# Layer 1 attention of a four-part transformer kernel: where VectorE's remainder of the turned probabilities stands in its queue, in the last step of a light head

## The chip, the cores and the metric

The kernel runs on one core of a Trainium2 chip. The core has TensorE (PE in the profile) for matrix products, VectorE (DVE), ScalarE (ACT), GpSimd (POOL) and SyncE (SP), which issues DMAs here. Each engine works through a queue of its own in the order in which the program put the instructions there, and engines wait for each other with semaphores. The metric is the device time of one execution in microseconds (us); lower is better. The time of the kernel before is 1416.83 us, the median of three runs (1416.50 to 1417.45).

## What is computed

Two transformer layers on 4 sequences of 256 tokens with 512 features, in float32. Only the attention of layer 1 is touched:

```
q = einsum('bsd,de->bse', x, wq).reshape(B, S, 32, 192)
k, v = 32 heads of 128 each out of x @ wkv
scores = einsum('bqhd,bkhd->bhqk', q[..., :128], k) * scale
scores = where(causal, scores, -1e30)
probs = softmax(scores, axis=-1)
attn = einsum('bhqk,bkhd->bqhd', probs, v)
out = einsum('bse,ed->bsd', attn, wo)
x = layernorm(x + out)
```

Before it stand layer 0 (attention, a gated feed-forward network) and behind it the last feed-forward part with its eight small experts.

## The kernel before

**Layout.** Tokens lie in 128-row tiles, two tiles to a sequence. A float32 operand of a product is held as two parts, a rounded one (`hi`) and the remainder (`lo`), and a product is three matmuls, hi x hi, hi x lo and lo x hi (`matmul3`, lines 106 to 108).

**Steps.** `programs` writes the attention of layer 1 as five functions, one for each engine. Each runs over 16 groups (`gr`), with two heads in each (`hd` 0 and 1, so head `h = 2 * gr + hd`) and four steps in each head (`t`, one for each sequence; the step number is `s = 4 * h + t`). Groups 1 to 14 are a loop, `Fori(1, NG - 1)`; group 0 and group 15 are written out apart. `light(gr, hd)` is true for the even head of the two groups that are written out, so for heads 0 and 30. In these, TensorE has less to do in a step than in the loop.

**What a step does.** The softmax of step `s + 1` is made while step `s` is at its products:

- TensorE: `scores(s + 1)` (lines 2240, 2241, 106 to 108 into `c_bs`), `turn(s)`, three transposes of the probabilities into `c_bt` (line 75), then products of the next head's queries and keys (`c_bx`, `c_by`), or of values or outputs (`c_bv`), and at the end `values(s)` (into `c_bo`). `turn(s)` waits for `s_norm`, which ScalarE raises when it has normalised the probabilities. `values(s)` waits for `s_tlo`, which VectorE raises when it has made the remainder of the turned probabilities.
- VectorE: `out_sum(s - 1)` (line 1999), `maxes(s + 1)`: the mask and the negated row maxima (lines 1977, 1978, 1981, 1983, 1985), `outs(s - 1)` (line 2006), `probs(s)`: the remainder `pt[1] = bt - pt[0]` (line 1993), `inverse(s + 1)` (line 1989), then parts of the next head.
- ScalarE: `out_rest(s - 1)` (line 1865), `probs(s)`: the rounded part `pt[0]` out of `bt` (line 1860), `outs(s - 1)` (line 1871), `exps(s + 1)` (line 1847), which waits for the maxima, `normalise(s + 1)` (line 1855), which waits for the reciprocals of `inverse`. In head 31 it also splits the weights of the last part there (line 2389).
- GpSimd splits the weights of the next heads.

Each function's text is the order of its engine's queue; no scheduler moves anything. In the last step (`t == 3`) of a light head VectorE's `probs(s)` already stands ahead of `outs(s - 1)`, behind `maxes(s + 1)`. These steps are `s = 3` (head 0) and `s = 123` (head 30).

The two places where such a step runs lie at 528 to 533 us and 1317 to 1322 us of the span.

Of the kernel before, what the change touches and what calls it, by code (L numbers as in the profile page):

```python
# [67 lines left out]
def f32(ap):  # L68

    return ap.bitcast(F32)  # L70
# [28 lines left out]
def has(x, n):  # L99

    return not isinstance(x, int) or 0 <= x < n
# [1443 lines left out]
class Attention1:  # L1545
# [128 lines left out]
    def programs(self, k, before, after, ffn0, end):  # L1674
# [8 lines left out]
        NSTEP = NB * NH  # L1683
# [41 lines left out]
        def in_last(gr):  # L1725
            return isinstance(gr, int) and gr == NG - 1

        def light(gr, hd):
            return isinstance(gr, int) and gr in (0, NG - 1) and hd == 0
# [241 lines left out]
        def vector(dve):  # L1971
            def maxes(s, t):


                dve.wait_ge(s_smm, s + 1)
                bank = bs[t % 2]
                dve.tensor_tensor(s0, bank[:, 3 * P:4 * P], mask, ALU.add).then_inc(s_mk, 1)
                dve.tensor_tensor(bank[:, 2 * P:3 * P], bank[:, 2 * P:3 * P], mask, ALU.add)\
                   .then_inc(s_mk, 1)
                dve.wait_ge(s_mk, 3 * s + 1)  # L1980
                dve.tensor_tensor(s0, bank[:, 0:P], s0, ALU.add).then_inc(s_mk, 1)
                dve.wait_ge(s_mk, 3 * s + 2)
                dve.tensor_reduce(nmax[t % 2][:, 1:2], bank[:, P:3 * P], AX, ALU.max, negate=True)
                dve.wait_ge(s_mk, 3 * s + 3)
                dve.tensor_reduce(nmax[t % 2][:, 0:1], s0, AX, ALU.max, negate=True).then_inc(s_max, 1)  # L1985

            def inverse(s, t):
                dve.wait_ge(s_exp, s + 1)
                dve.reciprocal(rinv[t % 2][:, :], rsum[t % 2][:, :]).then_inc(s_inv, 1)  # L1989

            def probs(s):
                dve.wait_ge(s_thi, s + 1)
                dve.tensor_tensor(pt[1], bt[:, 0:3 * P], f32(pt[0]), ALU.subtract).then_inc(s_tlo, 1)

            def out_sum(s, t):

                dve.wait_ge(s_orest, s + 1)
                out = bo[t % 2][:, P:2 * P]
                dve.tensor_tensor(out, out, o1, ALU.add).then_inc(s_osum, 1)  # L1999

            def outs(s, hd, b):
                dve.wait_ge(s_ohi, s + 1)
                tok = slice(b * S, (b + 1) * S)
                if isinstance(s, int) and s == 4 * (NH - 1):
                    dve.wait_ge(s_sumlo, 3 * NH)
                dve.tensor_tensor(out_home(s, 1, hd, tok), bo[b % 2][:, 0:S], f32(out_home(s, 0, hd, tok)),
                                  ALU.subtract).then_inc(s_olo, 1)

            def value_lo(n, b, bank):
                dve.wait_ge(s_vhi, n + 1)  # L2010
                dve.tensor_tensor(v[1][:, 2 * b:2 * b + 2, :], bank[:, :].rearrange("p (a n) -> p a n", a=2),
                                  f32(v[0][:, 2 * b:2 * b + 2, :]), ALU.subtract).then_inc(s_vlo, 1)

            def add_out(n, j, bank):

                dve.wait_ge(s_omm, n + 1)
                dve.tensor_tensor(res[:, j, :], bank[:, :], res[:, j, :], ALU.add).then_inc(s_oadd, 1)  # L2017

            def add_last(i):
                if i >= 14:  # L2020
                    dve.wait_ge(s_oadd, before_last + i - 1)
                add_out(before_last + i, last_tiles[i][1], last_banks[i])

            def last_stats(j):

                after.stats(dve, j, (s_oadd, before_last + last_tiles.index((B, j)) + 1))

            def total(h, i):

                n = (0, 2, 1)[i]  # L2030
                dve.wait_ge(s_y, 3 * h + i + 1)
                dve.wait_ge(s_copy, 3 * h + n + 1)
                if i == 1:
                    m = dve.tensor_tensor(y[:, n, :], by[:, :], y[:, n, :], ALU.add)
                else:
                    m = dve.scalar_tensor_tensor(out=y[:, n, :], in0=by[:, :], scalar=SCALE1, in1=y[:, n, :],  # L2036
                                                 op0=ALU.mult, op1=ALU.add)
                m.then_inc(s_sum, 1)

            def key_lo(h, par):  # L2040
                dve.wait_ge(s_khi, h + 1)
                dve.tensor_tensor(qk[par][:, 1, 1, 0:HALF], bx[:, :], f32(qk[par][:, 0, 1, 0:HALF]),
                                  ALU.subtract).then_inc(s_klo, 1)
# [59 lines left out]
            def unit(gr, hd):  # L2103
                h = 2 * gr + hd
                for t in range(NB):
                    s = 4 * h + t
                    if has(s - 1, NSTEP):
                        out_sum(s - 1, (t - 1) % 4)
                    if hd == 1 and t and has(gr + 1, NG):
                        value_lo(4 * gr + 4 + t - 1, t - 1, bv)  # L2110
                    if hd == 0 and t == 0 and not (isinstance(gr, int) and gr == 0):
                        value_lo(4 * gr + 3, 3, bv)
                    if has(s + 1, NSTEP):
                        maxes(s + 1, (t + 1) % 4)
                    few = light(gr, hd)
                    if few and t == 3:
                        probs(s)
                    if has(s - 1, NSTEP):
                        outs(s - 1, hd if t else 1 - hd, (t - 1) % 4)
                    if has(s, NSTEP) and not (few and t == 3):  # L2120
                        probs(s)
                    if few and t == 2:
                        key_lo(h + 1, 1 - hd)
                    if has(s + 1, NSTEP):
                        inverse(s + 1, (t + 1) % 4)
                    if hd == 0 and not in_last(gr) and has(gr - 1, NG):
                        add_out(8 * (gr - 1) + 2 * t, 2 * t, bv)
                    if t == 2 and has(h + 1, NH) and not few:
                        key_lo(h + 1, 1 - hd)
                    if t < 3 and has(h + 1, NH):  # L2130
                        total(h + 1, t)
                    if hd == 0 and not in_last(gr) and has(gr - 1, NG):
                        add_out(8 * (gr - 1) + 2 * t + 1, 2 * t + 1, bv if t < 3 else by)
                    if in_last(gr):
                        steps = last_steps.get((hd, t), ())
                        if hd == 1 and t == 2:
                            add_last(steps[0])
                            steps = steps[1:]
                        if hd == 1 and t >= 2:
                            for j in (2 * t - 4, 2 * t - 3):  # L2140
                                last_stats(j)
                            if t == 3:
                                after.spread(dve, 0, 4)
                        for i in steps:
                            add_last(i)

            def epilogue():
# [8 lines left out]
                end.vector(dve, (s_oadd, NT * NG))  # L2156

            sweep(dve, prologue, unit, epilogue)

        def tensor(pe):  # L2160
# [675 lines left out]
```

## Time and profile before

| | |
|---|---|
| Median of three runs | 1416.83 us (1416.50 to 1417.45) |
| The profiled execution, its own time | 1415.87 us |
| Its span, first to last instruction | 1414.1 us |
| Attention of layer 1, group 0 / loop / group 15 | about 511 to 560 / 560 to 1304 / 1304 to 1345 us |
| Mean granted TensorE clock | 0.999 of full speed |

The page gives busy time of each engine, the chain of work that ended last, and groups of instructions with their mean duration and the idle time ahead of them. A timeline view lists instructions of an engine by their start. In square brackets it gives the idle time of the engine ahead of an instruction and whose end it waited for. Matmuls overlap: the distance from start to start, and not the duration, is what each costs. The same holds on VectorE, where the next instruction's start can lie up to a tenth of a microsecond ahead of the end of the one before.

### The profile page before, as it was taken

How to read it: one execution, taken by the hardware profiler on the slowest of the kernel's cores; microseconds unless marked ns; L12 is line 12 of the kernel's file. 1: busy time of each engine (PE TensorE's matmuls, PEld its weight loads, DVE VectorE, ACT ScalarE, POOL GpSimd, SP SyncE). 2: the span in 40 equal slices, each digit the busy share in tenths (PEclk: the TensorE clock that was granted, in tenths of full speed). 3: DMA queues.
4: the chain of work that ended last, by engine and by line, in shares of the span. 5: the costliest groups of instructions: out<-in, count | busy, mean ns of one | idle time of the engine just before them, and what ended most of it. 6: DMA issues, size and time to landing. Idle time of an engine off the chain costs nothing.

```text
span 1414.1 us, 30207 instructions
## 1 busy us (share of the span) xinstructions
PE 1400.2 (99%) x8769; PEld 1236.6 (87%) x8769; DVE 1017.3 (72%) x2528; ACT 891.2 (63%) x2445; POOL 774.0 (55%) x828
## 2 busy tenths in 40 slices
PE   9999999999999999999999999999999999999998
PEld 7898889888788878889889889889889889889887
DVE  5999999999968875665665665665665665665776
ACT  5888888888555576555556556556556556556711
POOL 3555555555040467765765765665665665665521
PEclk9999999999999999999999999999999999999999
DMA  5533333322445301111101011001002001000201
GB/s 197 169 95 95 95 95 95 94 66 51 134 135 164 97 31 61 31 31 59 30 30 59 30 30 59 30 30 59 30 30 59 30 30 59 30 30 30 83 16 46
DMA packets 56155, 92.60 MB, mean 65 GB/s; under 512 B 6064, under 2 KB 27312, under 8 KB 56112
## 3 DMA queue, kind: packets, MB, share of 16 engines
q1 hardware_dynamic: 55968, 91.93, 21.3%
q8 instruction: 23, 0.38, 0.1%
q14 instruction: 20, 0.16, 0.0%
q10 hardware_dynamic: 144, 0.13, 0.0%
HBM read 81.82 MB, written 2.10 MB: 59 GB/s over the span
## 4 chain that ended last, share of the span: by engine, by line
PE 94%; DVE 2%; ACT 1%; issue 1%; POOL 1%; DMA 1%; SPq 0%; POOLq 0%; DVEq 0%; ACTq 0%
PE c_bv L106 8%; PE c_bv L108 7%; PE c_bv L107 7%; PE c_bx L106 5%; PE h_bo L944 5%; PE c_bx L108 4%; PE c_bx L107 4%; PE c_by L106 4%; PE c_by L108 4%; PE c_by L107 4%; PE h_bo L1447 3%; PE a_acc L1447 3%; PE h_bt L75 3%; PE h_bs L106 2%; PE c_bt L75 2%; PE h_bs L108 2%
## 5 line engine op out<-in xcount | busy, mean ns | idle before, releaser
L618 POOL TENSOR_TENSOR h_pr<-h_pr,h_rinv 128x512 f32<-128x512 f32 x128 | 133.2, 1041 | 136.7 <-DVE h_rinv L769 134.3
L1778 POOL TENSOR_TENSOR c_qk<-g_y,c_qk 128x512 fp32r<-128x512 f32 x96 | 124.0, 1292 | 147.3 <-ACT c_qk L1890 140.6
L1629 POOL TENSOR_TENSOR b_sw_lo<-b_slots,b_sw_hi 128x512 fp32r<-128x512 f32 (+1 forms) x128 | 148.1, 1157 | 10.2
L1627 POOL CAST b_sw_hi<-b_slots 128x512 fp32r<-128x512 f32 (+1 forms) x128 | 72.6, 567 | 143.6 <-DMA b_slots<-in_w_qk 125.5
L106 PE MATMUL c_bv<-b_wv_hi,g_xT_hi 128*128 128x256 f32 x496 | 138.8, 280 | 0.2 <-DVE g_xT_lo L1183 0.2
L108 PE MATMUL c_bv<-b_wv_hi,g_xT_lo 128*128 128x256 f32 x496 | 138.8, 280 | 0.0
L107 PE MATMUL c_bv<-b_wv_lo,g_xT_hi 128*128 128x256 f32 x496 | 138.7, 280 | 0.0
L1999 DVE TENSOR_TENSOR c_bo<-c_bo,g_wo 128x128 f32<-128x128 f32 x128 | 38.3, 300 | 122.3 <-ACT g_wo L1865 117.6
L1890 ACT ACTIVATE c_qk<-g_y 128x512 fp32r<-128x512 f32 x96 | 60.7, 632 | 96.5 <-DVE g_y L2036 67.1
L671 ACT ACTIVATE h_pr<-h_bs,h_nmax 128x256 f32<-128x256 f32 x256 | 119.3, 480 | 2.5 <-DVE h_nmax L764 2.4
L1855 ACT ACTIVATE c_pr<-c_pr,c_rinv 128x128 f32<-128x128 f32 (+1 forms) x256 | 101.8, 448 | 9.1 <-DVE c_rinv L1989 9.1
L1847 ACT ACTIVATE c_pr<-g_wo,c_nmax 128x128 f32<-128x128 f32 x128 | 51.5, 403 | 84.3 <-DVE c_nmax L1985 84.3
L107 PEld LDWEIGHTS c_bv<-b_wv_lo,g_xT_hi 128*128 128x128 f32 x496 | 93.1, 188 | 4.7
L106 PEld LDWEIGHTS c_bv<-b_wv_hi,g_xT_hi 128*128 128x128 f32 x496 | 93.0, 187 | 4.7 <-DVE g_xT_lo L1183 0.3
L1609 POOL TENSOR_TENSOR b_slots<-b_slots 128x256 f32<-128x256 f32 x128 | 93.8, 755 | 2.5
L108 PEld LDWEIGHTS c_bv<-b_wv_hi,g_xT_lo 128*128 128x128 f32 x496 | 93.1, 188 | 0.0
L2017 DVE TENSOR_TENSOR g_res<-c_bv,g_res 128x512 f32<-128x512 f32 x103 | 71.2, 692 | 27.2 <-PE c_bv L108 27.2
L764 DVE TENSOR_REDUCE h_nmax<-h_bs 128x2 f32<-128x512 f32 x128 | 87.5, 684 | 0.0
L773 DVE TENSOR_TENSOR h_pt_lo<-h_bt,h_pt_hi 128x512 fp32r<-128x512 f32 x128 | 87.2, 681 | 0.2
L1860 ACT ACTIVATE c_pt<-c_bt 128x384 fp32r<-128x384 f32 x128 | 62.9, 491 | 35.3 <-PE c_bt L75 31.5
L1865 ACT ACTIVATE g_wo<-c_bo 128x128 f32<-128x128 f32 x128 | 35.3, 276 | 77.3 <-PE c_bo L2262 77.3
L106 PE MATMUL c_bv<-b_wo_hi,c_oT 128*128 128x512 f32 x200 | 81.4, 407 | 0.0
(480 smaller groups left out, 5140.2 us busy)
## 6 DMA issues: line engine op xcount, KB each, us to landing
f_wi<-in_w_ffn SPq DMA_DIRECT2D x66, 256.0 KB, 2.7
b_slots<-in_w_qk SPq DMA_DIRECT2D x64, 256.0 KB, 3.0
a_w<-in_w_head SPq DMA_DIRECT2D x28, 352.0 KB, 2.9
h_part<-in_w_ffn SPq DMA_DIRECT2D x32, 264.0 KB, 2.7
b_raw_v<-in_w_v SPq DMA_DIRECT2D x16, 512.0 KB, 4.5
b_raw_o<-in_w_o SPq DMA_DIRECT2D x16, 512.0 KB, 4.5
h_o_mix<-h_o_hi SPq DMA_DIRECT2D x62, 128.0 KB, 2.2
b_ffn_w<-in_w_ffn SPq DMA_DIRECT2D x4, 576.0 KB, 5.6
```

Of the source, the lines that this page charges most:

```text
L106: pe.matmul(out, w[0], x[0], start=start, stop=False, skip_group_check=True)
L107: pe.matmul(out, w[0], x[1], start=False, stop=False, skip_group_check=True)
L108: return pe.matmul(out, w[1], x[0], start=False, stop=stop, skip_group_check=True)
L618: pool.tensor_tensor(pr[b][:, :, :], pr[b][:, :, :], rinv[b][:, :][:, :, None].to_broadcast([P, 2, S]), ALU.mult)\
L671: m = act.activation(pr[b][:, i, :], bs[b % 2][:, i * S:(i + 1) * S], ACT.Exp, bias=nmax[b][:, i:i + 1], accum_out=rsum[b][:, i:i + 1])
L764: dve.tensor_reduce(nmax[b][:, :], bs[b % 2][:, :].rearrange("p (a n) -> p a n", a=2), AX, ALU.max, negate=True).then_inc(s_max, 1)
L773: dve.tensor_tensor(pt[b][1][:, :, :], bt[b % 2][:, :].rearrange("p (a n) -> p a n", a=2), f32(pt[b][0][:, :, :]), ALU.subtract).then_inc( ...
L1447: m = pe.matmul(out, a, b, start=start and i == 0, stop=stop and i == len(pairs) - 1, skip_group_check=True)
L1609: pool.tensor_tensor(slot(out), slot(a), slot(b), op).then_inc(self.s_comb, 1)
L1629: pool.tensor_tensor(self.sw[1][:, a:b], self.slots[:, a:b], f32(self.sw[0][:, a:b]), ALU.subtract)\
L1778: pool.tensor_tensor(lo, src, f32(hi), ALU.subtract).then_inc(s_sumlo, 1)
L1855: m = act.activation(x[:, cols], x[:, cols], ACT.Identity, scale=rinv[t % 2][:, i:i + 1])
```

## The change

In the last step of a light head, VectorE's `probs(s)` (one instruction, line 1993 in both kernels, with its wait for `s_thi`) is placed ahead of `maxes(s + 1)` (five instructions) instead of behind it. No instruction is added or removed, and no other engine's order changes.

```
                         value_lo(4 * gr + 3, 3, bv)
-                    if has(s + 1, NSTEP):
-                        maxes(s + 1, (t + 1) % 4)
                     few = light(gr, hd)
                     if few and t == 3:
                         probs(s)
+                    if has(s + 1, NSTEP):
+                        maxes(s + 1, (t + 1) % 4)
                     if has(s - 1, NSTEP):
                         outs(s - 1, hd if t else 1 - hd, (t - 1) % 4)
```

`few and t == 3` holds twice: in group 0, step 3, and in group 15, step 123. VectorE's queue at the first place, in the kernel before (`c_bs0` are the scores of step 4, `c_bt` the turned probabilities of step 3, `c_bo0` the attention output of step 2, `g_wo` holds scratch):

```order
399 L1999 TENSOR_TENSOR c_bo0<-c_bo0,g_wo 128x128
400 L1977 TENSOR_TENSOR g_wo<-c_bs0,g_wo 128x128
401 L1978 TENSOR_TENSOR c_bs0<-c_bs0,g_wo 128x128
402 L1981 TENSOR_TENSOR g_wo<-c_bs0,g_wo 128x128
403 L1983 TENSOR_REDUCE c_nmax0<-c_bs0 128x1
404 L1985 TENSOR_REDUCE c_nmax0<-g_wo 128x1
405 L1993 TENSOR_TENSOR c_pt<-c_bt,c_pt 128x384
406 L2006 TENSOR_TENSOR c_oT<-c_bo0,c_oT 128x256
407 L1989 RECIPROCAL c_rinv0<-c_rsum0 128x2
```

And in the changed one:

```order
399 L1999 TENSOR_TENSOR c_bo0<-c_bo0,g_wo 128x128
400 L1993 TENSOR_TENSOR c_pt<-c_bt,c_pt 128x384
401 L1977 TENSOR_TENSOR g_wo<-c_bs0,g_wo 128x128
402 L1978 TENSOR_TENSOR c_bs0<-c_bs0,g_wo 128x128
403 L1981 TENSOR_TENSOR g_wo<-c_bs0,g_wo 128x128
404 L1983 TENSOR_REDUCE c_nmax0<-c_bs0 128x1
405 L1985 TENSOR_REDUCE c_nmax0<-g_wo 128x1
406 L2006 TENSOR_TENSOR c_oT<-c_bo0,c_oT 128x256
407 L1989 RECIPROCAL c_rinv0<-c_rsum0 128x2
```

The remainder of step 3 has moved past the masking and the maxima of step 4, five instructions. The second place, step 123, is the same on VectorE in the changed kernel (here `L2006` writes into the space of the value weights, and `L2017` adds output products to the residual):

```order
L1999 TENSOR_TENSOR c_bo<-c_bo,g_wo 128x128
L1993 TENSOR_TENSOR c_pt<-c_bt,c_pt 128x384
L1977 TENSOR_TENSOR g_wo<-c_bs,g_wo 128x128
L1978 TENSOR_TENSOR c_bs<-c_bs,g_wo 128x128
L1981 TENSOR_TENSOR g_wo<-c_bs,g_wo 128x128
L1983 TENSOR_REDUCE c_nmax<-c_bs 128x1
L1985 TENSOR_REDUCE c_nmax<-g_wo 128x1
L2006 TENSOR_TENSOR b_wv_lo<-c_bo,b_wv_hi 128x256
L1989 RECIPROCAL c_rinv<-c_rsum 128x2
L2017 TENSOR_TENSOR g_res<-c_bv,g_res 128x512
L2017 TENSOR_TENSOR g_res<-c_by,g_res 128x512
L1999 TENSOR_TENSOR c_bo<-c_bo,g_wo 128x128
```

Before, its L1993 stood between L1985 and L2006 there too.

## Rows read from the trace of the kernel before

**Rows 1.** The page, busy time: engine, busy us (share), instructions.

```profile
PE 1400.2 (99%) x8769; PEld 1236.6 (87%) x8769; DVE 1017.3 (72%) x2528; ACT 891.2 (63%) x2445; POOL 774.0 (55%) x828
```

**Rows 2.** The chain that ended last, first place: start us, us, what.

```profile
531.07 0.18 DVE c_rinv L1989
...
531.58 0.50 ACT c_pr L1855
532.12 0.45 PE c_bt L75 x3
```

**Rows 3.** Timeline of VectorE, first place: start us, us, instruction [idle before].

```profile
528.65 0.30 DVE L1999 TENSOR_TENSOR c_bo<-c_bo,g_wo 128x128 f32<-128x128 f32 x1 [0.96 <-ACT g_wo L1865]
528.86 0.28 DVE L1977 TENSOR_TENSOR g_wo<-c_bs,g_wo 128x128 f32<-128x128 f32 x1
...
529.78 0.28 DVE L1985 TENSOR_REDUCE c_nmax<-g_wo 128x1 f32<-128x128 f32 x1
529.98 0.55 DVE L1993 TENSOR_TENSOR c_pt<-c_bt,c_pt 128x384 fp32r<-128x384 f32 x1
530.44 0.41 DVE L2006 TENSOR_TENSOR c_oT<-c_bo,c_oT 128x256 fp32r<-128x256 f32 x1
```

**Rows 4.** Timeline of ScalarE, first place.

```profile
528.52 0.47 ACT L1860 ACTIVATE c_pt<-c_bt 128x384 fp32r<-128x384 f32 x1
...
530.09 0.40 ACT L1847 ACTIVATE c_pr<-g_wo,c_nmax 128x128 f32<-128x128 f32 x1 [0.72 <-DVE c_nmax L1985]
...
531.27 0.80 ACT L1855 ACTIVATE c_pr<-c_pr,c_rinv 128x128 f32<-128x128 f32 x2 [0.23 <-DVE c_rinv L1989]
```

**Rows 5.** Timeline of TensorE, first place.

```profile
529.51 0.40 PE L108 MATMUL c_bx<-g_xT_hi,b_sw_lo 128*128 128x512 f32 x1
530.62 0.35 PE L106 MATMUL c_bo<-c_pt,c_v_hi 128*128 128x256 f32 x1 [0.72 <-issue]
...
531.73 0.28 PE L108 MATMUL c_bs<-c_qk 128*128 128x256 f32 x1
532.12 0.45 PE L75 MATMUL c_bt<-g_ident,c_pr_t 128*128 128x128 f32 x3
```

**Rows 6.** Busy time by stretch: us, PE, PEld, DVE, ACT, POOL, clock, DMA, GB/s.

```profile
530.00:532.60 2.60, 1.84 (x13) 1.52 (x13) 1.02 (x4) 2.28 (x8) 2.52 (x4) 1.00 0.00 0
...
585.95:639.14 53.19, 53.19 (x334) 47.73 (x333) 32.95 (x93) 31.52 (x90) 33.61 (x34) 1.00 0.14 41
```

**Rows 7.** Timeline of VectorE, from the second place on.

```profile
1318.05 0.28 DVE L1977 TENSOR_TENSOR g_wo<-c_bs,g_wo 128x128 f32<-128x128 f32 x1
...
1319.17 0.55 DVE L1993 TENSOR_TENSOR c_pt<-c_bt,c_pt 128x384 fp32r<-128x384 f32 x1
...
1321.53 0.29 DVE L1999 TENSOR_TENSOR c_bo<-c_bo,g_wo 128x128 f32<-128x128 f32 x1
...
1333.25 0.41 DVE L2006 TENSOR_TENSOR g_o_last<-c_bo,g_o_last 128x256 fp32r<-128x256 f32 x1
```

**Rows 8.** Timeline of ScalarE, from the second place on.

```profile
1317.71 0.48 ACT L1860 ACTIVATE c_pt<-c_bt 128x384 fp32r<-128x384 f32 x1
...
1320.47 0.80 ACT L1855 ACTIVATE c_pr<-c_pr,c_rinv 128x128 f32<-128x128 f32 x2 [0.23 <-DVE c_rinv L1989]
...
1329.53 2.20 ACT L2389 ACTIVATE b_ffn_hi<-b_ffn_w 128x1152 fp32r<-128x1152 f32 x2
1331.64 0.25 ACT L1865 ACTIVATE g_wo<-c_bo 128x128 f32<-128x128 f32 x1
```

**Rows 9.** Timeline of TensorE, from the second place on.

```profile
1320.31 0.28 PE L106 MATMUL c_bo<-c_pt,c_v_hi 128*128 128x256 f32 x1
...
1321.48 0.37 PE L75 MATMUL c_bt<-g_ident,c_pr_t 128*128 128x128 f32 x3
...
1333.77 0.47 PE L106 MATMUL c_bx<-b_wo_last,b_wv_hi 128*128 128x512 f32 x1 [0.64 <-issue]
```

**Rows 10.** Busy time by stretch, end of the span (columns as in rows 6).

```profile
1411.00:1412.00 1.00, 0.00 (x0) 0.00 (x0) 0.63 (x2) 0.00 (x0) 0.00 (x0) 0.50 0.13 41
```

More of the change, by code:

```diff
@@ L2112, in unit @@
                         value_lo(4 * gr + 3, 3, bv)
-                    if has(s + 1, NSTEP):
-                        maxes(s + 1, (t + 1) % 4)
                     few = light(gr, hd)
@@ L2117, in unit @@
                         probs(s)
+                    if has(s + 1, NSTEP):
+                        maxes(s + 1, (t + 1) % 4)
                     if has(s - 1, NSTEP):
```

## The prediction

> **What bounds the kernel now.** I read the busy times first. TensorE is busy 99% of the span [rows 1], so an edit on VectorE can matter only at the few places where TensorE stands still. In the loop it never does: one pass of two heads takes 53.19 us and TensorE is busy for all of it [rows 6]. That has a second meaning. TensorE does not catch up there, so a delay at the loop's entry is carried to its end, and a gain would be too.
>
> Then the two places of the change. At the first, TensorE has two holes in 2.6 us [rows 5]. Its last product of the next head starts at 529.51 and holds it to about 529.74, since such matmuls follow each other every 0.23 us. `values(3)` starts at 530.62, a hole of 0.88 us. The second hole is ahead of `turn(4)`: the last matmul of `scores(5)` starts at 531.73, is over by 531.85, and the transposes start at 532.12, 0.27 us later.
>
> The first hole ends with VectorE's L1993: it starts at 529.98 and ends at 530.53 [rows 3], 0.09 us ahead of TensorE's start. The second ends with ScalarE's normalisation, from 531.27 to 532.07 [rows 4]. The chain of waits goes through the second only [rows 2]: reciprocal, normalisation, transposes. It goes back from there over the exponentials at 530.09, which had waited 0.72 us for the maxima of L1985 [rows 4]. The first hole, though three times as long, isn't in it: had `values(3)` been earlier, `turn(4)` would still have started at 532.12.
>
> **Place one, step 3.** The change moves one instruction, L1993, ahead of five. Without the five in front it waits only for ScalarE's rounded part, L1860, which ends at 528.99 [rows 4]. The handover between these engines takes 0.03 us (L1985 ends at 530.06, ScalarE starts at 530.09 [rows 3, 4]), so L1993 starts at 529.02 and ends at 529.57, instead of 530.53. `values(3)` can then start when TensorE is free, at 529.74. The hole of 0.88 us is gone.
>
> The price stands behind it in VectorE's queue. The mask and the maxima started at 528.86 [rows 3]. Now they start when L1993 lets the next one in. L1993 holds the queue for 0.46 us, from 529.98 to 530.44 in before [rows 3], so that is 529.02 + 0.46 = 529.48. They are 0.62 us later: 0.16 us in which VectorE now waits for ScalarE, and 0.46 us of L1993. Queued behind the waiting L1993 are just these five, and ScalarE's exponentials wait for them. L2006 comes 0.16 us later and nobody waits for it within a microsecond. The reciprocal waits for the exponentials anyway.
>
> From the maxima on every link is tight: the exponentials go from 530.09 to 530.71, the normalisation ends at 532.69 instead of 532.07, and `turn(4)` starts at 532.74 instead of 532.12. TensorE is through with `values(3)` and `scores(5)` at about 530.97, and has one hole of 1.77 us in place of 0.88 and 0.27. Net: **0.62 us lost**. Behind `turn(4)`, ScalarE's copy for the next head, which TensorE's next product needs, comes after the normalisation and moves by the same 0.62. Then TensorE runs without a hole into the loop, and the loss is carried [rows 6].
>
> Bounds. Below: nothing, if a link I call tight has room; a gain needs the maxima not to move, and in one queue behind L1993 they must. Above: 0.71 us, if the next instruction starts only at L1993's end (0.55 instead of 0.46 us). I take 0.62, since the spacing of 0.46 is a row.
>
> The Trainium skill has a rule for this, in VectorE: DVE Perf Modes, section The DRAIN you can't avoid: the next op doesn't start until the pipe of the one before has emptied. By it the loss would be 0.71 us at each place and the sum 0.18 us more. The row speaks against it, as L2006 starts 0.09 us before L1993 ends.
>
> A second page looks at the holes themselves. Perfetto Trace Analysis, section Optimization Strategy, says to find the gaps on the bounding engine, see which semaphore each waits for, and make that dependency start sooner. Applied to the longest gap it is this very change, and it would promise 0.88 us gained. It doesn't say that the gap behind it may be the one that counts here.
>
> **Place two, step 123.** Here TensorE has six output products of 512 columns for each of two tiles between `turn(123)` and `values(123)`. `values(123)` starts at 1320.31 [rows 9] and L1993 ended at 1319.72 [rows 7], so 0.6 us of room: an earlier L1993 buys nothing at all. The maxima move as before. L1860 ends at 1318.19 [rows 8], L1993 starts at 1318.22 and lets them in at 1318.68 instead of 1318.05 [rows 7]: 0.63 us later.
>
> The normalisation of step 124 ended at 1321.27 [rows 8], now at 1321.90. The transposes would start at 1321.95 instead of 1321.48 [rows 9], so TensorE gets a new hole of 0.47 us there. Of the 0.63, 0.16 was room. That is the lower bound at this place.
>
> The remaining 0.16 is lost a little later. VectorE and ScalarE have next to no room in the last group. After the maxima of step 124 VectorE works back to back up to L1999 at 1321.53 [rows 7], since it adds output products to the residual. In each of the next steps ScalarE splits a piece of weights between normalisation and L1865. The longest is the pair from 1329.53, and L1865 starts behind it at 1331.64 with no idle time [rows 8]. The maxima of the last step and L2006 at 1333.25 [rows 7] hang on that L1865. L2006 ends at 1333.66, and the product that needs its output starts at 1333.77, with TensorE idle for 0.64 us ahead of it [rows 9]. So TensorE waits for VectorE there, VectorE is 0.63 us late by a chain without room, and the product starts at 1334.40. Both losses are one and the same: at 1333.77 the sum of place two is **0.63 us**, the 0.47 within it. After that everything again waits for TensorE.
>
> **The sum.** No instruction is added, no DMA, no wait that wasn't there. 0.62 + 0.63 = 1.25 us. The profiled execution has a span of 1414.1 us and its own time is 1415.87, 1.77 more. It becomes a span of 1415.35 and 1417.1 us. The median of the three runs lies 0.96 us above the profiled execution, so the forecast for a median is 1416.83 + 1.25 = **1418.1 us**, 0.09% more. A measurement here can tell 0.2% from no change, 2.8 us, so this counts as the same.
>
> **The rivals.**
>
> 1. Only place one costs, since somewhere in the long chain of the last group there is room that I didn't see: 0.62, 1417.45 us. For it speaks the length of that chain, 15 us over four steps. Against it, each link's idle time is short. 16%.
> 2. Nothing is lost or the two effects cancel (also: the edit doesn't change what the engines do in time, since L1993 waits for ScalarE until close to its old place): 1416.8 us. The rows speak against it, L1860 is over 0.99 us before L1993's old start [rows 3, 4]. 6%.
> 3. The longest hole decides: 0.88 us gained at place one, nothing lost: 1415.95 us. It needs `turn(4)` to start earlier, though the chain ties it to maxima that come later [rows 2]. 4%.
> 4. Slower by more than can be overlooked: the new hole of 1.77 us at 531 lets TensorE's clock fall. The granted clock is 1.00 in the stretch with both old holes [rows 6], and 0.50 (the 1.2 GHz level) in a stretch without any TensorE work at the end of the span, from 1411 us on [rows 10], 3.1 us before the span ends. If the hole brought as many microseconds, 3.1, at half the clock, products would lose half of it, 1.55 us, giving 1416.83 + 1.25 + 1.55 = 1419.6. From 3.2 us at half the clock on, the loss passes 2.8 us in all, at 1419.7. Against it: TensorE is busy for 1.84 of the 2.6 us around the two old holes at a clock of 1.00 [rows 6], and would be for only some 0.6 us less. 5%.
>
> **How the numbers follow.** The forecast has 66%, the rivals 31% together, and 3% is left for what I don't see. The range: its low end takes in rival 1 with a median at the low side by the 0.96 us that the profiled execution lies below the median, 1416.5. Its high end is the forecast plus the same amount, 1419.0; the bound of 0.71 us for each place is within it. That leaves rivals 3 and 4 out. Faster by over 0.2% would need 2.8 us, and both holes of place one together are 1.15: 1%. Slower by over 0.2% is rival 4 at its worse half and the unseen: 4%. The same: 95%.
>
> **What would show it.** Right: L1993 at about 529.02 and 1318.22 with a short idle time ahead of it that ScalarE's L1860 ended; `values(3)` starting straight behind the products; transposes of step 4 at about 532.74 with one hole of some 1.8 us ahead; each loop pass still 53.19 us; a new hole of 0.47 us ahead of the transposes of step 124; and the hole at the product for tile 2 growing from 0.64 to 0.8 us (0.16 of the loss falls there). Wrong: `turn(4)` at or before 532.12, or a span under 1414.6 or over 1416, or a granted clock under 1.00 around 532.

## The result, and the profile after

The changed kernel takes 1419.4 us, the median of 22 runs (1417.32 to 1421.34), against 1416.91 us for the kernel before (22 runs, 1416.20 to 1417.53). That is 2.49 us more. The ratio is 1.0016 with a 95% interval of 1.0010 to 1.0022. By 0.2% it still counts as no change, but it is twice the 1.25 us forecast, and its range of 1416.5 to 1419.0 missed it.

The spread tells more than the median: 4.0 us where the kernel before has 1.3. Sorted, the 22 runs part into 10 from 1417.32 to 1418.83 (median 1418.28, 1.37 over before) and 12 from 1419.24 up (median 1420.06, 3.15 over before). In the first ten the mean granted clock is 0.999, but for one at 0.998. In the other twelve it is 0.998 or 0.997 (rounded values, which order the runs only roughly). So the median lies between two kinds of execution 1.8 us apart, of which only the first is what the sum described. The border isn't sharp, with 0.41 us between the last of the one and the first of the other; it is the one that the experiments below use, 2 us over the median of before.

The profiled execution is one of the first kind: 1418.53 us, clock 0.999. VectorE at the first place (start us, us, instruction, idle before), to be held against [rows 3]:

```profile
529.30 0.30 DVE L1999 TENSOR_TENSOR c_bo<-c_bo,g_wo 128x128 f32<-128x128 f32 x1 [0.96 <-ACT g_wo L1865]
529.68 0.56 DVE L1993 TENSOR_TENSOR c_pt<-c_bt,c_pt 128x384 fp32r<-128x384 f32 x1
530.16 0.28 DVE L1977 TENSOR_TENSOR g_wo<-c_bs,g_wo 128x128 f32<-128x128 f32 x1
...
532.37 0.17 DVE L1989 RECIPROCAL c_rinv<-c_rsum 128x2 f32<-128x2 f32 x1 [0.68 <-ACT c_pr L1847]
```

Everything in this trace is 0.65 us later already at L1999, in a part of the program that the change doesn't touch; that belongs to the single execution. Counted from L1999, the maxima begin 0.86 us on instead of 0.21, 0.65 us later. TensorE at the same place, to be held against [rows 5]:

```profile
530.13 0.39 PE L108 MATMUL c_bx<-g_xT_hi,b_sw_lo 128*128 128x512 f32 x1
530.36 0.34 PE L106 MATMUL c_bo<-c_pt,c_v_hi 128*128 128x256 f32 x1
...
531.47 0.28 PE L108 MATMUL c_bs<-c_qk 128*128 128x256 f32 x1
533.43 0.45 PE L75 MATMUL c_bt<-g_ident,c_pr_t 128*128 128x128 f32 x3 [1.68 <-ACT c_pr L1855]
533.91 0.50 PE L106 MATMUL c_bx<-b_ts,b_sw_hi 128*128 128x512 f32 x1
```

The first hole is closed: the values follow 0.23 us behind the last product. In place of the two holes of before there is one ahead of the transposes, shown as 1.68 us. Counted from L1999 again, the transposes stand at 4.13 us instead of 3.47 (532.12 less 528.65 in [rows 5, 3]): 0.66 us lost. The chain of waits now goes through L1993 at 529.68 itself:

```profile
529.27 0.39 ACT c_pt L1860
...
529.68 0.56 DVE c_pt L1993
...
530.83 0.33 DVE c_nmax L1983
...
531.39 0.96 ACT c_pr L1847 x4
...
532.88 0.50 ACT c_pr L1855
...
533.43 0.45 PE c_bt L75 x3
...
533.91 0.50 PE c_bx L106
```

A pass of the loop is as long as before [rows 6]:

```profile
587.23:640.42 53.19, 53.19 (x334) 47.73 (x333) 32.95 (x93) 31.54 (x90) 33.62 (x34) 1.00 0.13 40
```

TensorE at the second place, to be held against [rows 9]:

```profile
1322.65 0.28 PE L108 MATMUL c_bs<-c_qk 128*128 128x256 f32 x1
1323.25 0.45 PE L75 MATMUL c_bt<-g_ident,c_pr_t 128*128 128x128 f32 x3 [0.33 <-ACT c_pr L1855]
...
1335.70 0.47 PE L106 MATMUL c_bx<-b_wo_last,b_wv_hi 128*128 128x512 f32 x1 [0.76 <-issue]
```

There is a new hole ahead of the transposes of step 124 (0.60 us from start to start, where back to back it is 0.12), and the hole at the product for tile 2 has grown from 0.64 to 0.76. From the transposes of step 4 to this product it takes 802.27 us instead of 801.65, so 0.62 us are lost here. The two places together make 1.28. The span is 2.5 us longer, 1416.6: 0.65 from before the first place, 1.28 from the change, and 0.6 behind the last computation, in the output's way to memory.

### The profile page after: what moved, and what is told of

Read it like the earlier page. It is cut to its first block, busy times and chain, and to the rows that moved or that the text cites. A ratio compares the mean times of both kernels' runs of the same rounds, so it can differ in the third digit from the quotient of the medians.

```text
span 1416.6 us, 30207 instructions
## 1 busy us (share of the span) xinstructions
PE 1400.1 (99%) x8769; PEld 1236.4 (87%) x8769; DVE 1017.4 (72%) x2528; ACT 891.9 (63%) x2445; POOL 774.5 (55%) x828
## 4 chain that ended last, share of the span: by engine, by line
PE 92%; DVE 3%; ACT 2%; issue 1%; POOL 1%; DMA 1%; SPq 0%; POOLq 0%; DVEq 0%; ACTq 0%
PE c_bv L106 7%; PE c_bv L108 7%; PE c_bv L107 7%; PE h_bo L944 5%; PE c_bx L106 5%; PE c_bx L108 4%; PE c_bx L107 4%; PE c_by L106 4%; PE c_by L108 3%; PE c_by L107 3%; PE h_bo L1447 3%; PE a_acc L1447 3%; PE h_bt L75 3%; PE h_bs L106 2%; PE h_bs L108 2%; PE h_bs L107 2%
## 5 line engine op out<-in xcount | busy, mean ns | idle before, releaser
L1999 DVE TENSOR_TENSOR c_bo<-c_bo,g_wo 128x128 f32<-128x128 f32 x128 | 38.4, 300 | 122.6 <-ACT g_wo L1865 120.1
L2017 DVE TENSOR_TENSOR g_res<-c_bv,g_res 128x512 f32<-128x512 f32 x103 | 71.2, 691 | 27.1 <-PE c_bv L108 27.1
```

## The experiments

Each experiment ran 11 times beside the kernel before. "Late" in the table counts the runs that lie more than 2 us over the median of the kernel before in the same set. The kernel before ran 33 times beside e1 to e4, 33 beside e5 to e8, 21 beside e9 and e10 and 21 beside e11 and e12 (medians 1417.17, 1417.22, 1416.97 and 1416.95 us); one of these 108 runs was late. Each ratio comes with its 95% interval. A time alone doesn't say why a run is late; the traces do, one for each row. The expectations weigh four theories: M (only the moved maxima), K (the clock falls at place one), L (it falls in the last group) and T (the time is lost behind the last product).

| | median us | over before | range | late | ratio |
|---|---|---|---|---|---|
| e1 changed kernel again | 1419.28 | +2.11 | 1418.14 to 1421.35 | 6 of 11 | 1.0016 (1.0007 to 1.0025) |
| e2 first place alone | 1418.22 | +1.05 | 1417.19 to 1419.65 | 3 of 11 | 1.0009 (1.0000 to 1.0018) |
| e3 second place alone | 1417.87 | +0.70 | 1417.05 to 1418.52 | 0 | 1.0005 (0.9996 to 1.0014) |
| e4 changed, hole filled | 1418.22 | +1.05 | 1417.25 to 1418.70 | 0 | 1.0007 (0.9998 to 1.0016) |
| e5 changed, remainder later still | 1420.55 | +3.33 | 1419.85 to 1421.52 | 11 of 11 | 1.0025 (1.0016 to 1.0034) |
| e6 changed, hole partly filled | 1418.34 | +1.12 | 1417.94 to 1419.45 | 2 of 11 | 1.0010 (1.0001 to 1.0019) |
| e7 maxima first, heads 0 and 30 | 1416.77 | -0.45 | 1416.25 to 1417.09 | 0 | 0.9997 (0.9988 to 1.0006) |
| e8 maxima first, head 0 | 1416.88 | -0.34 | 1416.11 to 1418.57 | 0 | 0.9999 (0.9990 to 1.0008) |
| e9 before, maxima later | 1417.69 | +0.72 | 1417.05 to 1418.11 | 0 | 1.0004 (0.9995 to 1.0013) |
| e10 maxima and exponentials first | 1416.31 | -0.66 | 1415.91 to 1417.42 | 0 | 0.9996 (0.9987 to 1.0005) |
| e11 before, maxima later still | 1418.15 | +1.20 | 1417.45 to 1420.36 | 3 of 11 | 1.0010 (1.0001 to 1.0019) |
| e12 as e10 | 1416.53 | -0.42 | 1415.64 to 1418.27 | 0 | 0.9997 (0.9988 to 1.0006) |

**The changed kernel once more (e1).** No edit.

> The changed kernel once more. Theory M (moved maxima only): every run is about 1.25 us over the kernel before, a spread as narrow as before's (1.3 us), granted clock 0.999 in each. Theory K (clock): on top of M the hole ahead of the transposes of step 4 lets TensorE's granted clock fall in a part of the executions: those at a mean clock of 0.999 lie about 1.2 us over before, those at 0.998 or 0.997 2.5 to 4 us over, and a trace of one of these shows 0.50 in a stretch behind 533 us. Theory T (tail): the clock is 1.00 up to 1410 us in every execution and the spread comes from the time between the last product and the end of the output transfers.

The profile caught an execution of the second kind (1420.06 us, clock 0.997). TensorE, behind the same hole as above:

```profile
533.10 0.45 PE L75 MATMUL c_bt<-g_ident,c_pr_t 128*128 128x128 f32 x3 [1.68 <-ACT c_pr L1855]
533.58 0.63 PE L106 MATMUL c_bx<-b_ts,b_sw_hi 128*128 128x512 f32 x1
534.01 0.63 PE L107 MATMUL c_bx<-b_ts,b_sw_hi 128*128 128x512 f32 x1
...
538.04 0.39 PE L106 MATMUL c_by<-g_xT_hi,b_sw_hi 128*128 128x512 f32 x1
```

Products of 512 columns follow each other every 0.43 us instead of 0.23. And the busy time by stretch (columns as in rows 6):

```profile
530.00:533.50 3.50, 1.82 (x14) 1.52 (x13) 1.53 (x7) 2.20 (x8) 3.42 (x4) 1.00 0.00 0
533.50:534.00 0.50, 0.47 (x2) 0.33 (x2) 0.28 (x2) 0.50 (x3) 0.50 (x2) 0.81 0.00 0
534.00:537.00 3.00, 3.00 (x11) 2.51 (x10) 2.09 (x9) 1.39 (x6) 2.92 (x4) 0.50 0.02 5
537.00:537.50 0.50, 0.50 (x5) 0.50 (x5) 0.00 (x0) 0.38 (x1) 0.50 (x2) 0.78 0.00 0
537.50:540.00 2.50, 2.50 (x18) 2.24 (x17) 0.38 (x1) 0.91 (x3) 1.39 (x2) 1.00 0.00 0
```

The granted clock is 1.00 in the hole and falls to 0.50, the level of 1.2 GHz, only when TensorE is at work again; it is back at about 537.2, so the low level lasts 3.4 us (0.81 and 0.78 in the half microseconds at its ends stand for 0.19 and 0.22 us of it). The stretch from the first product behind the transposes to the queries' product in c_by takes 4.46 us (533.58 to 538.04). In the kernel before the same 18 matmuls take 2.87:

```profile
532.61 0.50 PE L106 MATMUL c_bx<-b_ts,b_sw_hi 128*128 128x512 f32 x1
...
535.48 0.39 PE L106 MATMUL c_by<-g_xT_hi,b_sw_hi 128*128 128x512 f32 x1
```

They take 2.87 in the changed kernel's other trace too (533.91 to 536.78). So the clock costs 1.59 us. Behind it nothing more is lost: from that product in c_by to the transposes of step 123 this trace has 781.74 us and the other 781.69. Up to 1410 us the clock is 1.00 everywhere else in this trace. Of the 11 runs 6 are late, five of them with a mean clock of 0.998 or 0.997; the sixth, 2.11 over before at 0.999, may be scatter. Theory K stands.

The same look at all 14 traces, before, after and the twelve experiments: the four of late runs (e1, e2, e5, e11) have the clock down once, at 534 to 538 us, and the other ten have it at 1.00 in every 10 us up to 1410. T is out, since a time behind the last product can't slow products at 534 us, and M is only the lower part.

The Trainium skill describes such a gate in TensorE: Matmul & The Clock Gate, section What's actually happening: a block that watches how busy the array has lately been decides how many clock pulses pass, half of them after idleness. The two levels and the fall behind the hole agree with the trace. No run here shows what it watches.

**The first place alone (e2).**

> Only step 3 (head 0) has the remainder ahead of the maxima; step 123 stands as in the kernel before. Theory M: 0.62 us over before, narrow. Theory K: 0.62 us over before in the best runs, up to 3.5 us in those with a mean clock of 0.997 or 0.998, since the hole of 1.77 us is there; median some 1.5 to 2 us over before. If the clock falls at step 123 instead (theory L): narrow, as M.

```
-                    if few and t == 3:
+                    if few and t == 3 and gr == 0:
                         probs(s)
                     if has(s + 1, NSTEP):
                         maxes(s + 1, (t + 1) % 4)
+                    if few and t == 3 and not gr == 0:
+                        probs(s)
```

Eight runs lie at 0.0 to 1.4 us over before, three at 2.2 to 2.5, and the profile is of one of the three: the hole ends at 533.35 and the clock is 0.83 in the stretch from 534 to 535 us, 0.50 from 535 to 538 and 0.96 in the next. Here the two kinds are there without the second place. The median was expected higher, at 1.5 to 2 over before: 3 of 11 runs are late, where 12 of 22 and 6 of 11 are in the changed kernel. With so few runs that difference isn't settled.

**The second place alone (e3).** The same edit with `gr == NG - 1`.

> Only step 123 (head 30) has the remainder ahead of the maxima; step 3 stands as in the kernel before. Theory M and theory K: 0.63 us over before, narrow, clock 0.999 in every run. Theory L (the clock falls in the last group, where TensorE gets a hole of 0.47 and one of 0.8 us): wide, with runs at 0.997 and 0.998.

0.70 us over before, no late run. The interval of its ratio doesn't leave out 1, but the trace has the cost: from the transposes of step 123 to the product for tile 2 it takes 17.22 us (1317.42 to 1334.64) instead of 16.59, so 0.63 more. Place two costs what the sum said and brings no clock loss, so theory L is out. In the trace the transposes of step 124 wait as in the changed kernel, and so does the product for tile 2:

```profile
1322.20 0.45 PE L75 MATMUL c_bt<-g_ident,c_pr_t 128*128 128x128 f32 x3 [0.35 <-ACT c_pr L1855]
...
1334.64 0.47 PE L106 MATMUL c_bx<-b_wo_last,b_wv_hi 128*128 128x512 f32 x1 [0.72 <-issue]
```

**The hole filled (e4).** Seven matmuls whose result nobody reads, on the changed kernel.

> The changed kernel with seven extra matmuls of 512 columns (1.6 us, into the bank c_bv, which holds nothing then) in the hole ahead of the transposes of step 4. They fit in the hole and add no result. Theory K: 1.25 us over before (up to 0.2 more if the last ends after the probabilities are normalised), narrow, clock 0.999 in every run. Theories M, T: no change against the changed kernel, so wide as it is, with runs 2.5 us and more over before.

```
+                    if isinstance(gr, int) and gr == 0 and hd == 1 and t == 0:
+                        for i in range(7):
+                            pe.matmul(bv[:, :], xhi[:, 0, 0:P], xhi[:, 0, 0:HALF], start=True, stop=True, ...)
                     turn(s, t)
```

Same waits, more work for TensorE, and 1.06 us faster than the changed kernel in the same set (1418.22 against 1419.28). None of 11 runs is late, against 6 of 11; the slowest is 1.53 us over before. TensorE's timeline in its trace shows the matmuls in the hole:

```profile
530.94 1.78 PE L2315 MATMUL c_bv<-g_xT_hi 128*128 128x512 f32 x7
532.78 0.45 PE L75 MATMUL c_bt<-g_ident,c_pr_t 128*128 128x128 f32 x3
```

The busy time by stretch of the same trace shows the clock at 1.00:

```profile
534.00:537.00 3.00, 3.00 (x21) 2.70 (x20) 1.78 (x7) 1.12 (x6) 2.92 (x4) 1.00 0.02 5
```

In the 3 us from 534 TensorE starts 21 matmuls; with the clock down it had started 11. This is the experiment that parts the clock from the waiting: the transposes are as late as in the changed kernel, 4.13 us behind L1999 in both traces, and the extra loss is gone. What is left, 1.05, is the 1.25 of the sum within the scatter of such medians.

**The remainder later still (e5).**

> The changed kernel with one more VectorE instruction ahead of the remainder of step 3: a maximum over 384 columns of c_bt into a scratch column that nobody reads, estimated at 0.46 us in the queue from the 0.33 us of the one over 256 columns. Queue arithmetic alone (theory M): the hole ahead of the transposes of step 4 grows from 1.7 to about 2.1 us, 1.7 us over the kernel before, narrow. Theory K (the hole lets the clock fall in part of the executions, 1.6 us each time): it falls in more executions than in the changed kernel or for longer, median 3 to 3.5 us over before, the best runs 1.7 over.

```
                 dve.wait_ge(s_thi, s + 1)
+                if isinstance(s, int) and s == 3:
+                    dve.tensor_reduce(g["wo"][:, 3 * P:3 * P + 1], bt[:, 0:3 * P], AX, ALU.max)
                 dve.tensor_tensor(pt[1], bt[:, 0:3 * P], f32(pt[0]), ALU.subtract).then_inc(s_tlo, 1)
```

All 11 runs are late, in a band of only 1.7 us; the lowest is 2.63 over before, where the sum alone has 1.72. The median of 3.33 us over before is 1.72 (the sum with one more instruction of 0.47) and 1.61 for the clock, which is the 1.59 read from e1's trace. The one expectation that missed is the hole: it did not grow to 2.1 us in one piece, since the values wait for the remainder as well. TensorE's timeline:

```profile
530.82 0.36 PE L106 MATMUL c_bo<-c_pt,c_v_hi 128*128 128x256 f32 x1 [0.28 <-issue]
...
533.90 0.62 PE L75 MATMUL c_bt<-g_ident,c_pr_t 128*128 128x128 f32 x3 [1.69 <-ACT c_pr L1855]
534.39 0.80 PE L106 MATMUL c_bx<-b_ts,b_sw_hi 128*128 128x512 f32 x1
```

It has 0.28 and 1.69 us. With the large hole as long as in the changed kernel and only a small one added ahead of it, all 11 runs are late and not every other one.

**The hole partly filled (e6).** As e4 with `range(3)`.

> The changed kernel with three extra matmuls of 512 columns (0.7 us) ahead of the transposes of step 4, instead of seven. TensorE still stands still for about 1.0 us in one piece. Theory K with the idle time in sum as the measure (the kernel before had 1.15 us there in two pieces and its clock stayed up): clock falls in no execution, 1.25 us over before, narrow. If one hole of 1 us is enough whatever the sum: some runs at 2.8 us over before.

The trace shows 0.98 us of idle time ahead of the transposes, a clock of 1.00, and the median is where the sum has it, 1.12 over before. Two runs are at 2.1 and 2.2 over before and so count as late, at mean clocks of 0.999 and 1.000, so they do not look like clock losses. What they are stays open.

**The maxima later, in the order of before (e9 and e11).** Does the place of the idle time matter, or the order of the change? These two leave the order of the kernel before and delay the maxima of step 4 with one or two instructions that compute nothing needed.

> The order of the kernel before, with one more VectorE instruction (a maximum over 384 columns into a scratch column that nobody reads, 0.47 us in the queue) ahead of the masking of step 4. The maxima of step 4 are about as late as in the changed kernel (0.47 against 0.62 us) but the remainder of step 3 is late too, so TensorE's idle time of 1.6 us stays in two pieces, about 1.35 ahead of the values and 0.27 ahead of the transposes. Theory M: 0.47 us over before. Theory K with the idle time in sum as the measure: a part of the executions loses another 1.6 us, as in the changed kernel, so median 0.5 to 1.5 over before and the slowest runs 2 us over. Theory K with one long hole as the measure: as the sum gives, 0.47 over, narrow.

> As e9_late_max with two such VectorE instructions instead of one. TensorE's idle time is then about 2.1 us there, 1.8 us ahead of the values of step 3 and 0.3 us ahead of the transposes of step 4, so as much in sum as in e5_longer (0.3 and 1.8 us), in which every run lost the extra 1.6 us, and with one hole as long as in the changed kernel. Queue arithmetic alone (theory M): 0.94 us over before, narrow. Theory K: the clock falls in many or all executions here too, though the maxima and not the remainder were delayed: median 2 to 2.6 us over before. If it stays up in all of them, something other than the idle time (the place at the transposes) decides.

```
                 dve.wait_ge(s_smm, s + 1)
                 bank = bs[t % 2]
+                if isinstance(s, int) and s == 4:
+                    dve.tensor_reduce(g["wo"][:, 3 * P:3 * P + 1], f32(xhi[:, 0, 0:3 * P]), AX, ALU.max)
```

With one, the idle time is 1.21 us ahead of the values and 0.27 ahead of the transposes, and none of 11 runs is late: 0.72 over before for 0.46 in the queue, and for 0.46 in the trace from one step's transposes to the next's (4.59 us instead of 4.13). With two, TensorE's timeline shows:

```profile
532.25 0.36 PE L106 MATMUL c_bo<-c_pt,c_v_hi 128*128 128x256 f32 x1 [1.64 <-issue]
...
533.76 0.58 PE L75 MATMUL c_bt<-g_ident,c_pr_t 128*128 128x128 f32 x3
534.24 0.79 PE L106 MATMUL c_bx<-b_ts,b_sw_hi 128*128 128x512 f32 x1
534.83 0.63 PE L107 MATMUL c_bx<-b_ts,b_sw_hi 128*128 128x512 f32 x1
```

Now 3 of 11 are late, and the trace, of one of them, has the clock at 0.50 from 534 to 537, the very place as in e1. So the clock loss does not need the moved remainder; enough idle time of TensorE around 531 us brings it, ahead of the transposes as in e1 or ahead of the values as here. The median of 1.20 is under the 2 to 2.6 expected, though. With nearly the idle time of e5 (1.64 and 0.27 us against 0.28 and 1.69) the clock seems to have fallen 3 times where it fell 11 times out of 11. Either these few hundredths matter, or the order of the holes and the work between them does; no run parts the two. Against the changed kernel's 18 of 33 the difference may be chance.

**Maxima ahead of the output sum (e7 and e8).** If the maxima decide, VectorE should take them before the instruction ahead of them that waits for ScalarE.

> From the kernel before: in the steps of heads 0 and 30 the masking and maxima of the next step stand ahead of the output sum of the step before, which waits for ScalarE; the remainder stays where it was. At step 3 the maxima start at about 528.1 instead of 528.9, the remainder ends 0.6 us earlier, and the exponentials, which stand behind ScalarE's copy of the last output, start 0.2 us earlier. Theory of the chain (softmax of the next step decides): 0.2 to 1.0 us less than before over the eight steps, narrow, clock 0.999. If the order in which VectorE serves the two does not matter: the same as before.

> As the run before, but in head 0 alone; head 30 keeps the order of the kernel before. Theory of the chain: 0.2 to 0.5 us less than before. In head 30 TensorE has no hole ahead of step 125, so the other run should not be much better than this one, except by the delay ahead of the product for tile 2 (0.64 us idle), which hangs on VectorE and ScalarE.

```
+                    few = light(gr, hd)
+                    if has(s + 1, NSTEP) and few:
+                        maxes(s + 1, (t + 1) % 4)
                     if has(s - 1, NSTEP):
                         out_sum(s - 1, (t - 1) % 4)
...
-                    if has(s + 1, NSTEP):
+                    if has(s + 1, NSTEP) and not few:
                         maxes(s + 1, (t + 1) % 4)
```

VectorE at step 3 of the kernel with both heads:

```profile
528.90 0.29 DVE L1977 TENSOR_TENSOR g_wo<-c_bs,g_wo 128x128 f32<-128x128 f32 x1 [0.30 <-PE c_bs L108]
...
530.03 0.29 DVE L1999 TENSOR_TENSOR c_bo<-c_bo,g_wo 128x128 f32<-128x128 f32 x1
530.23 0.55 DVE L1993 TENSOR_TENSOR c_pt<-c_bt,c_pt 128x384 fp32r<-128x384 f32 x1
```

The masking now waits for TensorE's scores and for nothing else, and neither L1999 nor the remainder has idle time ahead of it. In the traces the transposes of step 4 start 3.76 (e7) and 3.75 us (e8) behind those of step 3, instead of 4.13 in the kernel before (532.12 less 527.99). Both medians are lower than before, by 0.45 and 0.34 us, as the chain had it, but no interval leaves 1 out: the traces show the gain at this place, the times only suggest it.

**Exponentials ahead of the output copy, too (e10 and e12).**

> The kernel with the maxima ahead of the output sum in heads 0 and 30, and besides, at step 3 alone, ScalarE's exponentials of step 4 ahead of its copy of the last output, VectorE's reciprocal ahead of its remainder of that output. Theory of the chain: the exponentials start at about 529.3 instead of 529.9, the transposes of step 4 at about 531.4 instead of 531.9, TensorE's hole ahead of them shrinks from 0.4 to 0.2 us or less, 0.8 to 1.0 us less than before. If something else ends last there: the same as the run with the maxima ahead of the output sum, 0.45 us less than before.

> The kernel of e10_exps_first once more, for the size of its gain: if it was real, again 0.5 to 0.8 us less than before; if that was scatter of the medians, within 0.3 us of before.

```
+                    exps_first = light(gr, hd) and gr == 0 and t == 3
+                    if exps_first:
+                        exps(s + 1, (t + 1) % 4)
                     if has(s - 1, NSTEP):
                         outs(s - 1, hd if t else 1 - hd, (t - 1) % 4)
...
-                    if has(s + 1, NSTEP):
+                    if has(s + 1, NSTEP) and not exps_first:
                         exps(s + 1, (t + 1) % 4)
```

On VectorE `inverse(4)` stands ahead of `outs(2)` to match. The medians are 0.66 and 0.42 us under before, less than the 0.8 to 1.0 expected; the repeat, between the 0.3 and the 0.5 of its expectation, settles nothing, and neither is clear of e7's 0.45. In e10 the transposes of step 4 start 3.29 us behind those of step 3 (528.21). Then TensorE runs into another engine, as its timeline shows:

```profile
531.50 0.45 PE L75 MATMUL c_bt<-g_ident,c_pr_t 128*128 128x128 f32 x3
532.43 0.47 PE L106 MATMUL c_bx<-b_ts,b_sw_hi 128*128 128x512 f32 x1 [0.48 <-POOL b_sw_lo L1629]
```

GpSimd's split of the next head's weights ends last there. From the transposes of step 3 to this product it takes 4.22 us in e10 and 4.24 in e7, against 4.62 in the kernel before, so the exponentials bring nothing more at the product. In e12's trace the hole for GpSimd is 1.17 us and the stretch 4.89, longer than before. A further gain at this place would have to come from GpSimd; that wasn't tried.

## Why the prediction was wrong

**What held.** The bounding engine, and the rule that a loss at the loop's entry is carried: each pass is still 53.19 us. Place one: the first hole closed, the maxima 0.62 us later by the sum and 0.65 by the trace, the transposes 0.66 later. The hole of 1.77 us is 1.84 by the same measure, from 531.59 to 533.43. L1993 held the queue for 0.48 us instead of 0.46. Place two: a new hole of 0.47 by the sum, 0.48 by the trace, and 0.63 by the sum against 0.62 at the product for tile 2 (0.76 us of idle time for 0.8). The sum of 1.25 us is 1.28 in the trace and 1.37 in the lower ten runs. Queue arithmetic from the rows was right to a few hundredths.

**What failed.** The step is the clock: the sum put TensorE's clock at nothing, and the fourth rival, which had it, got 5%. Its mechanism was the right one, and the loss shows in the times of 12 of 22 executions (6 of 11 in the repeat), 1.59 us each by e1's trace. Its price of 1.55 us came near by luck: the 3.1 us at half the clock were what was left of the span behind 1411 us, and not how long the clock stays down, which is 3.4 us in e1. The argument against it was that TensorE was busy for 1.84 us of the 2.6 around the old holes at a clock of 1.00, and would be for only some 0.6 less. (That row also begins inside the first hole, 0.26 us behind its start.) "Only" was not read from anything: a row that shows the clock up at one amount of work says nothing on how near that is to a fall. e9 and e11 show how near it was: 0.46 us more of delay and no run is late, twice that and 3 of 11 are.

A second mistake follows from it. The rival was priced as a case of its own that either holds or doesn't. It is a mixture within one kernel, part of the executions with the loss and part without. For a median the share matters, and a share near one half puts it in between. The range, 1416.5 to 1419.0, held only the lower kind and left the other out. To hold a median at any share it would have had to reach to the second kind's own, 1420.06.

Two of the recorded signs of being wrong came. The profiled span is 1416.6, over 1416, though 1.25 of its 2.5 us lie outside the change. And the clock is under 1.00 in e1, not at 532 in the hole but from 533.8 on.

**The other rivals.** That only place one costs: e3 shows 0.63 us for place two alone in its trace, 0.70 in its median. Nothing lost, or 0.88 gained: out, by the trace, where the first hole closed and the transposes came later all the same. The rule on VectorE's pipe (the Trainium skill, VectorE: DVE Perf Modes, The DRAIN you can't avoid) would have had the masking start 0.56 us behind L1993's start; it starts 0.48 us behind. The same section adds that a next op that is not held starts earlier, and with that the trace agrees. The advice of the Trainium skill, Perfetto Trace Analysis, section Optimization Strategy, to make the dependency of a gap start sooner, needs an order here: the gap to serve was the shorter one. e7 serves it, with 0.37 us gained at the transposes in its trace.

## What to carry to other kernels

In one queue, an instruction moved ahead of others delays them all by its wait and its length, here five by 0.65 us. So before closing TensorE's longest hole, look at which hole the chain of waits goes through: here 0.88 us were won ahead of one product and 0.66 net were lost ahead of the next. When an edit merges or lengthens holes of TensorE, give the fall of its clock a real chance, price it from the two levels, and look at the spread of the runs and the mean clock of each, since one profile can show either kind. If work without a result placed in the hole brings time back, and the trace has the clock up there, it was the clock.

## What the runs showed of the hardware that was not expected

- One hole of 1.7 us ahead of the transposes of step 4 goes with late runs in 18 of 33 of the changed kernel, and with 0.28 us more of idle time a little ahead of it in 11 of 11 (e5).
- The clock fell late: 1.00 through the hole, and 0.50 from about 533.8 us on, 0.7 us after the work had begun again, up to 537.2 (e1). In e2 it fell more than a microsecond after the hole's end, in e5 right at it. In all four traces that show it (e1, e2, e5, e11) the low level lies between 533.8 and 538.1 us and lasts 3.4 us, wherever it begins. It costs 1.59 us by e1's trace and 1.61 by e5's median.
- Seven matmuls more made the changed kernel 1.06 us faster (e4 against e1).
- The kernel before is close to that edge: with its maxima 0.9 us later 3 of 11 runs were late (e11), with 0.46 none (e9). What exactly tips it, and why the share differs between e2 and the changed kernel, is open.
